# Emitting the next token group's load and normalization in pieces between the pieces of the current group's projections

## The chip, the cores and the metric

One Trainium2 chip, all 8 of its cores, one launch. Each core runs the same program on its own share and never waits for another. The metric is device time in microseconds (us) of the slowest core. The engines are TensorE (PE), VectorE (DVE), ScalarE (ACT), GpSimd (POOL) and SyncE (SP, which only issues DMAs here); each takes its instructions in order.

## The reference

One transformer block on x of 4 x 4096 x 2048: latent attention, then a gated feed-forward with int8 weights.

```python
h = layernorm(x)
q = h @ Wq + bq
kv_latent = h @ Wdown            # 2048 -> 512
k = kv_latent @ Wk_up            # 512 -> 2048
v = kv_latent @ Wv_up
q, k = rope(q), rope(k)          # 16 heads of 128
attn = softmax(causal(q k^T / sqrt(128)))
x = x + layernorm((attn v) @ Wo + bo)
g = silu((layernorm(x) @ w_gate) * s_gate)
u = (layernorm(x) @ w_up) * s_up
x = x + layernorm(((g * u) @ w_down) * s_down)
```

## The kernel before

Two cores share a batch row: each computes k and v for all 4096 tokens of it, and q, attention and feed-forward for 2048 of them. The program runs through stages A (normalization, latent, k, v), B (q), C (attention), D (output projection) and E (feed-forward), with a barrier of all engines behind each. Only stage A is touched by the change.

The program is first written down as lists, one for each engine: every call of `st(engine, fn, waits, ...)` appends one operation to its engine's list with the semaphore values that it waits for, and the lists are replayed in that order. So the order in which the Python code calls `st` is the order of each engine's queue, DMAs of SyncE among them; there is no other scheduler. Slots carry the events of a tile's last producer and of its users. SyncE's DMAs use eight semaphores in turn, and each waits for the one eight before it.

Stage A goes over 8 token groups (NKG) of 512 tokens. For each group:

- front(kg): four token tiles of 128. For each: SyncE loads x (line 337, 1 MB); VectorE sums (348); ScalarE squares and accumulates (350); small operations on VectorE, POOL and ScalarE give mean, variance, root (362) and reciprocal (364); ScalarE writes the normalized tile in bf16 (368); SyncE sends a transposing DMA that puts it into the group's feature-major tile xnfm (378). At the end two stores of xnfm to xnf_scr, 1 MB each (393), which wait for all four transposes. x tiles, normalized tiles and xnfm are double-buffered; the statistics are not.
- back(kg): the down projection, 4 chunks of 16 matmuls (411), each cast on ScalarE (420); then k, 16 chunks of 4 matmuls (442), each with three VectorE operations for the rotation (468, 470, 477) and a POOL add into the staging tile kst (485), and two stores to k_scr by SyncE (502); then v, 16 chunks of 4 matmuls (442 as well), each copied by ScalarE into vst (455), and two stores to v_scr (502). The chunks use two PSUM banks in turn.

The loop is `for kg in range(NKG): front(kg); back(kg)`, at the end of stage A.

Of the kernel before, what the change touches and what calls it, by code (L numbers as in the profile page):

```python
# [24 lines left out]
NKG = 8  # L25
# [89 lines left out]
def prod_waits(*slots):  # L115
    ws = []
    for s in slots:
        ws.extend(s.users)
        ws.extend(s.ready)
    return ws  # L120


def cons_waits(*slots):
    ws = []
    for s in slots:
        ws.extend(s.ready)
    return ws


def build_program():  # L130
# [120 lines left out]
    if "A" in PHASES:  # L251
# [74 lines left out]
        def front(kg):  # L326
            kgp = kg % 2
            xnfm = xnfm2[kgp]
            s_xnfm = s_xnfm2[kgp]
            for tt4 in range(4):  # L330
                tpar = (kg * 4 + tt4) % 2
                xt, sxt = x_t[tpar], s_xt[tpar]
                xn, sxn = xn_tm[tpar], s_xntm[tpar]
                row0 = kg * 512 + tt4 * 128

                ev = st("Q", lambda q, xt=xt, row0=row0:
                        q.dma_start(xt, xin[row0:row0 + 128, :]),
                        waits=prod_waits(sxt), dma="dQ")
                sxt.produced(ev)

                ssum = st_s[:, 0:1]
                nmean = st_s[:, 1:2]
                ssq = st_s[:, 2:3]
                var = st_s[:, 3:4]
                sd = st_s[:, 4:5]
                rstd = st_s[:, 5:6]
                t1 = st_s[:, 6:7]
                ev1 = st("V", lambda v, xt=xt: v.reduce_sum(ssum, xt, axis=AX),
                         waits=cons_waits(sxt) + prod_waits(s_stats))
                ev2 = st("S", lambda s, xt=xt: s.activation(  # L350
                    sqs, xt, ACT.Square, accum_out=ssq),
                    waits=cons_waits(sxt) + [ev1])
                sxt.used(ev2)
                ev3 = st("V", lambda v: v.tensor_scalar(
                    nmean, ssum, -1.0 / DM, None, op0=ALU.mult), waits=[ev1])
                ev4 = st("V", lambda v: v.tensor_scalar(
                    var, ssq, 1.0 / DM, None, op0=ALU.mult), waits=[ev2])
                ev5 = st("G", lambda g: g.tensor_mul(
                    t1, nmean, nmean), waits=[ev3])
                ev6 = st("G", lambda g: g.tensor_sub(var, var, t1),  # L360
                         waits=[ev4, ev5])
                ev7 = st("S", lambda s: s.activation(
                    sd, var, ACT.Sqrt, bias=eps_s, scale=1.0), waits=[ev6])
                ev8 = st("V", lambda v: v.reciprocal(rstd, sd), waits=[ev7])
                nmr = st_s[:, 7:8]
                ev8b = st("G", lambda g: g.tensor_mul(nmr, nmean, rstd),
                          waits=[ev8])
                ev9 = st("S", lambda s, xt=xt, xn=xn: s.activation(
                    xn, xt, ACT.Identity, bias=nmr, scale=rstd),
                    waits=prod_waits(sxn) + [ev8b])  # L370
                sxt.used(ev9)
                sxn.produced(ev9)
                s_stats.produced(ev8)
                s_stats.used(ev9)

                if tt4 == 0:
                    xnfm_evs = []
                ev = st("Q", lambda q, xn=xn, tt4=tt4, xnfm=xnfm: q.dma_start(
                    xnfm[:, :, tt4 * 128:(tt4 + 1) * 128], xn, transpose=True),
                    waits=cons_waits(sxn) + (prod_waits(s_xnfm)  # L380
                                             if tt4 == 0 else []),
                    dma="dQ", xpose=True)
                sxn.used(ev)
                xnfm_evs.append(ev)
            s_xnfm.produced(xnfm_evs)
            ev_xnfm = xnfm_evs

            for half in range(2):
                def fn(q, half=half, kg=kg, xnfm=xnfm):
                    dap = bass.AP(xnf_scr.tensor,  # L390
                                  half * 8 * 128 * SEQ + kg * 512,
                                  [[SEQ, 128], [128 * SEQ, 8], [1, 512]])
                    return q.dma_start(dap, xnfm[:, half * 8:half * 8 + 8, :])
                ev = st("Q", fn, waits=list(ev_xnfm), dma="dQ")
                s_xnfm.used(ev)
                scr_slot["xnf"].produced(ev)

        def back(kg):
# [5 lines left out]
            for lc in range(4):  # L404
                bank = lc % 2
                pss, psa = ps_slot[bank], ps_ap[bank]

                def fn(t, lc=lc, psa=psa, xnfm=xnfm):
                    r = None
                    for fc in range(NH):  # L410
                        r = t.matmul(psa, wdn_s[:, fc, lc * 128:(lc + 1) * 128],  # L411
                                     xnfm[:, fc, :],
                                     start=(fc == 0), stop=(fc == NH - 1))
                    return r
                ev = st("T", fn, waits=prod_waits(pss) +
                        cons_waits(s_xnfm, s_wdn))
                pss.produced(ev)
                s_xnfm.used(ev)
                s_wdn.used(ev)
                evv = st("S", lambda s, lc=lc, psa=psa, kvl=kvl: s.copy(  # L420
                    kvl[:, lc, :], psa),
                    waits=cons_waits(pss) + (prod_waits(s_kvl)
                                             if lc == 0 else []))
                pss.used(evv)
                if lc == 3:
                    s_kvl.produced(evv)
                elif lc == 0:
                    s_kvl.users = []

            for which in ("k", "v"):  # L430
                wsl = s_wku if which == "k" else s_wvu
# [1 line left out]
                stg = kst if which == "k" else vst  # L433
                sstg = s_kst if which == "k" else s_vst
                for fc in range(NH):
                    bank = 2 + (fc % 2)
                    pss, psa = ps_slot[bank], ps_ap[bank]

# [58 lines left out]
                for half in range(2):  # L497
                    def fn(q, dst=dst, half=half, stg=stg, kg=kg):
                        dap = bass.AP(dst.tensor,
                                      half * 8 * 128 * SEQ + kg * 512,  # L500
                                      [[SEQ, 128], [128 * SEQ, 8], [1, 512]])
                        return q.dma_start(dap, stg[:, half * 8:half * 8 + 8, :])
                    ev = st("Q", fn, waits=cons_waits(sstg), dma="dQ")
                    sstg.used(ev)
                    scr_slot[sname].produced(ev)

        for kg in range(NKG):
            front(kg)
            back(kg)

        plan.barrier()

# [771 lines left out]
```

How the kernel before makes its waits and increments, by code:

```python
    def replay(self, eng_handle, eng_name, sems):  # L85
        cur = {}
        for ws, fn, sem, inc in self.ops[eng_name]:
            for s, v in ws:
                if cur.get(s, 0) < v:
                    eng_handle.wait_ge(sems[s], v)
                    cur[s] = v
            if fn is None:
                continue
            inst = fn(eng_handle)
            if inc:
                inst.then_inc(sems[sem], inc)
```

## Time and profile before

| | us |
|---|---|
| median of 3 runs | 6654.31 |
| lowest run | 6634.15 |
| profiled execution, device time | 6641.46 |
| its span on the slowest core (core 2) | 6639.9 |
| spans of all cores | 6587.8 to 6639.9 |
| granted TensorE clock, all cores | 0.836 to 0.840 |

| stage | from, to (us of the span) |
|---|---|
| tables and weight preparation | 0 to 160 |
| stage A, first x load to last v store | 160 to 1315 |
| stage B | 1315 to 1600 |
| the rest | 1600 to 6640 |

PE is busy for 66% of the span, DVE 24%, ACT 20%, POOL 12%. A busy share is an average over stages with different limits, and stage A is where the page's slices show PE at 3 to 5 tenths. Durations of matmuls in the page overlap each other; their start-to-start distance is what they cost.

### The profile page before, as it was taken

To read this page: it belongs to the slowest core of one execution; us is meant where nothing else is said; L and a number is where in the kernel's file an instruction comes from. 1 tells how busy PE (TensorE), PEld (TensorE's weight loads), DVE (VectorE), ACT (ScalarE), POOL (GpSimd) and SP (SyncE) were. 2 spreads that over 40 slices of the span, in tenths; PEclk is the share of its full clock that TensorE was granted. 3 is DMA by queue.
4 is the path that set the end of the run, shared out by engine and by line. 5 is a ranking of instruction groups with operands and counts; after the bars stand their busy time and mean duration, and the time that the engine had idled before them with its cause. 6 is when DMAs were issued, how large, how long until landed. Compare 5 with 4: busy or idle time off the path is not lost.

```text
span 6639.9 us, 67786 instructions; the slowest of 8 cores (6587.8 to 6639.9 us)
## 1 busy us (share of the span) xinstructions
PE 4399.2 (66%) x21376; PEld 2013.5 (30%) x21376; DVE 1584.7 (24%) x2965; ACT 1349.2 (20%) x3067; POOL 818.8 (12%) x924
## 2 busy tenths in 40 slices
PE   0333434358566666663332999879986999869986
PEld 0111111123233333331111444334432444324432
DVE  0222333235233333323332111021102111021101
ACT  0222112111565666631111000011100100010000
POOL 0111111124000000000000111111111111111111
PEclk9866767679677666776776999989998999989998
DMA  9333323351777777774436997499956997489944
GB/s 187 94 86 91 86 76 89 105 111 39 164 151 149 154 153 149 149 160 127 139 114 129 153 153 142 127 165 152 146 140 153 154 153 133 128 162 152 153 122 131
DMA packets 1566328, 883.21 MB, mean 133 GB/s; under 512 B 777122, under 2 KB 1541026, under 8 KB 1550242
## 3 DMA queue, kind: packets, MB, share of 16 engines
q0 software_dynamic: 679296, 434.14, 38.2%
q1 hardware_dynamic: 839842, 327.28, 22.1%
q10 hardware_dynamic: 46848, 117.45, 5.3%
q8 instruction: 187, 3.06, 0.2%
q14 instruction: 155, 1.27, 0.1%
HBM read 398.53 MB, written 109.05 MB: 76 GB/s over the span
## 4 chain that ended last, share of the span: by engine, by line
PE 45%; DMA 19%; DVE 11%; ACT 11%; issue 8%; POOL 3%; SPq 2%; another core or an unknown queue 1%; ACTq 0%; DVEq 0%; POOLq 0%
PE ps L1029 13%; PE ps L1043 13%; PE ps L1096 8%; DMA arena<-wd 7%; ACT arena L764 7%; DMA ctxr<-xin 3%; PE ps L862 3%; PE ps L411 2%; PE ps L442 2%; PE ps L736 2%; DVE smalls L758 2%; POOL arena L619 2%; DMA arena<-arena 2%; DVE arena L477 1%; PE ps L697 1%
## 5 line engine op out<-in xcount | busy, mean ns | idle before, releaser
L1029 PE MATMUL ps<-arena 128*128 128x512 bf16 x4096 | 933.1, 381 | 265.4 <-DMA arena<-wg 142.5
L1096 PE MATMUL ps<-arena 128*128 128x512 bf16 x4096 | 916.5, 380 | 141.1 <-DMA arena<-wd 140.0
L1043 PE MATMUL ps<-arena 128*128 128x512 bf16 x4096 | 925.8, 379 | 0.0
L764 ACT ACTIVATE arena<-ps,smalls 128x512 bf16<-128x512 f32 (+1 forms) x1152 | 747.7, 666 | 461.6 <-DVE smalls L758 331.1
L736 PE MATMUL ps<-arena 128*128 128x512 bf16 (+1 forms) x1152 | 486.5, 485 | 418.6 <-ACT arena L764 337.7
L411 PE MATMUL ps<-arena 128*128 128x512 bf16 x512 | 128.8, 419 | 762.8 <-DMA arena<-ctxr 762.8
L1029 PEld LDWEIGHTS ps<-arena 128*128 128x128 bf16 x4096 | 402.1, 98 | 755.3 <-issue 277.1
L1096 PEld LDWEIGHTS ps<-arena 128*128 128x128 bf16 x4096 | 387.1, 98 | 669.9 <-issue 239.5
L1059 DVE TENSOR_SCALAR ctxr<-ps,smalls 128x512 bf16<-128x512 f32 x256 | 192.2, 751 | 1499.2 <-PE ps L1043 1499.2
L1043 PEld LDWEIGHTS ps<-arena 128*128 128x128 bf16 x4096 | 400.8, 98 | 483.2
L1054 ACT ACTIVATE ctxr<-ps,smalls 128x512 bf16<-128x512 f32 x256 | 175.9, 687 | 1562.6 <-PE ps L1029 1562.5
L862 PE MATMUL ps<-arena 128*128 128x512 bf16 x1024 | 227.7, 386 | 335.2 <-DMA arena<-wo_scr 306.7
L697 PE MATMUL ps<-arena 128*128 128x128 bf16 x4352 | 402.9, 267 | 30.2 <-DMA arena<-arena 22.6
L697 PEld LDWEIGHTS ps<-arena 128*128 128x128 bf16 x4352 | 364.6, 123 | 74.4 <-issue 63.3
L442 PE MATMUL ps<-arena 128*128 128x512 bf16 x1024 | 288.3, 419 | 126.5 <-DVE arena L477 116.1
L736 PEld LDWEIGHTS ps<-arena 128*128 128x128 bf16 x1152 | 117.4, 109 | 728.7 <-issue 721.9
L411 PEld LDWEIGHTS ps<-arena 128*128 128x128 bf16 x512 | 53.5, 106 | 837.6 <-issue 789.0
L585 PE MATMUL ps<-arena,ctxr 128*128 128x512 bf16 x1024 | 230.8, 390 | 113.6 <-DMA arena<-xnf_scr 85.2
L1085 POOL DMA_DIRECT2D arena<-wd x256 | 189.7, 741 | 943.6 <-PE ps L1096 932.0
L1019 POOL DMA_DIRECT2D arena<-wg x128 | 146.3, 1143 | 1165.2 <-PE ps L1029 1158.6
L1116 DVE TENSOR_TENSOR ctxr<-ps,ctxr 128x512 f32<-128x512 f32 x64 | 43.9, 691 | 1010.5 <-PE ps L1096 1010.3
L1148 ACT ACTIVATE sqs<-ctxr 128x2048 bf16<-128x2048 f32 x16 | 30.5, 1909 | 1166.8 <-DVE smalls L1145 1166.8
(74 smaller groups left out, 2781.5 us busy)
## 6 DMA issues: line engine op xcount, KB each, us to landing
arena<-wg POOLq DMA_DIRECT2D x128, 1024.0 KB, 6.8
arena<-wu POOLq DMA_DIRECT2D x128, 1024.0 KB, 7.1
arena<-wd POOLq DMA_DIRECT2D x256, 512.0 KB, 3.8
ctxr<-xin SPq DMA_DIRECT2D x32, 1024.0 KB, 5.9
arena<-wo_scr ACTq DMA_DIRECT2D x16, 2048.0 KB, 10.4
xnf_scr<-arena SPq DMA_DIRECT2D x16, 1024.0 KB, 7.1
k_scr<-ctxr SPq DMA_DIRECT2D x16, 1024.0 KB, 7.1
v_scr<-ctxr SPq DMA_DIRECT2D x16, 1024.0 KB, 7.5
```

Of the source, the lines that this page charges most:

```text
L411: r = t.matmul(psa, wdn_s[:, fc, lc * 128:(lc + 1) * 128], xnfm[:, fc, :], start=(fc == 0), stop=(fc == NH - 1))
L442: r = t.matmul(psa, wts[:, lc, fc * 128:(fc + 1) * 128], kvl[:, lc, :], start=(lc == 0), stop=(lc == 3))
L585: rr = t.matmul(psa, wq_s[:, fc, oc * 128:(oc + 1) * 128], xnfmB[:, fc, :], start=(fc == 0), stop=(fc == NH - 1))
L697: r = t.matmul(cpa[:, 0:128], PT_b[par][:, kc, :], v_t[hp][:, kc, :], start=(kc == 0), stop=(kc == W // 128 - 1))
L736: t.matmul(psa[:, 0:N], q_s[hp][:, tt * 128:(tt + 1) * 128], k_s[hp][:, n0:n0 + N], start=True, stop=True),
L764: s.activation(P_b[par][:, n0:n0 + N], psa[:, 0:N], ACT.Exp, bias=negc[:, par:par + 1], scale=1.0, accum_out=lacc[:, par * 8 + ci: par * 8 ...
L862: r = t.matmul(psa, ctxfm[tp][:, fc, j * 128:(j + 1) * 128], wo_s[wop][:, fc, :], start=(fc == 0), stop=(fc == NH - 1))
L1029: rr = t.matmul(ga, wg_s[slp][:, fc, icw * 128:(icw + 1) * 128], x1nfm[:, fc, :], start=(fc == 0), stop=(fc == NH - 1))
L1043: rr = t.matmul(ua, wu_s[slp][:, fc, icw * 128:(icw + 1) * 128], x1nfm[:, fc, :], start=(fc == 0), stop=(fc == NH - 1))
L1059: ev2 = st("V", lambda v, ic=ic, ua=ua: v.tensor_scalar(u_sb, ua, su_s[:, ic:ic + 1], None, op0=ALU.mult), waits=cons_waits(ub) + prod_wai ...
L1085: return g.dma_start(wd_s[qp], sap)
L1096: rr = t.matmul(psa, f_b[:, quar * 4 + ic, j * 128:(j + 1) * 128], wd_s[qp][:, ic, :], start=(quar == 0 and ic == 0), stop=(quar == 15 and ...
```

## The change

front and back become generators. front yields behind each token tile, and its two xnf stores come after the fourth yield. back yields behind the down projection, in the middle of k, behind the k stores, in the middle of v and behind the v stores. The driver runs front(0) by itself, and then for each group takes a piece of back(kg) and a piece of front(kg + 1) in turn. No operation, tile, wait rule or size differs; only the order in which the operations are put into the engines' lists.

```diff
@@ front(kg)
                 sxn.used(ev)
                 xnfm_evs.append(ev)
+                yield
             s_xnfm.produced(xnfm_evs)
             ev_xnfm = xnfm_evs
@@ back(kg)
                 elif lc == 0:
                     s_kvl.users = []
+            yield
 
             for which in ("k", "v"):
...
                 for fc in range(NH):
+                    if fc == 8:
+                        yield
                     bank = 2 + (fc % 2)
...
                     sstg.used(ev)
                     scr_slot[sname].produced(ev)
-
+                yield
+
+        def run_all(g):
+            for _ in g:
+                pass
+
+        fr = front(0)
+        run_all(fr)
+        fr = front(1) if NKG > 1 else iter(())
         for kg in range(NKG):
-            front(kg)
-            back(kg)
+            bk = back(kg)
+            while True:
+                try:
+                    next(bk)
+                except StopIteration:
+                    break
+                try:
+                    next(fr)
+                except StopIteration:
+                    pass
+            run_all(fr)
+            fr = front(kg + 2) if kg + 2 < NKG else iter(())
```

## Rows read from the trace of the kernel before

**Rows 1.** The page, costliest groups: busy, mean ns, idle before and its releaser.

```profile
L411 PE MATMUL ps<-arena 128*128 128x512 bf16 x512 | 128.8, 419 | 762.8 <-DMA arena<-ctxr 762.8
L442 PE MATMUL ps<-arena 128*128 128x512 bf16 x1024 | 288.3, 419 | 126.5 <-DVE arena L477 116.1
```

**Rows 2.** Table of stages: front(1), then down, k, v of back(1).

```profile
core 2: us, PE busy (x) PEld busy (x) DVE busy (x) ACT busy (x) POOL busy (x), PEclk, DMA share, GB/s
304.00:378.00 74.00, 0.31 (x1) 0.14 (x2) 11.03 (x16) 17.56 (x16) 2.30 (x12) 0.52 0.42 114
...
382.00:394.00 12.00, 11.87 (x55) 5.15 (x53) 0.00 (x0) 1.79 (x4) 0.00 (x0) 0.99 0.23 78
394.00:430.00 36.00, 21.23 (x68) 6.18 (x68) 32.57 (x48) 0.55 (x1) 19.03 (x15) 0.86 0.00 0
430.00:446.00 16.00, 14.50 (x62) 4.91 (x60) 0.53 (x1) 9.19 (x16) 1.27 (x1) 1.00 0.40 131
```

**Rows 3.** Timeline of PE: start, duration, what; first down matmuls of groups 1, 7.

```profile
377.69 16.18 PE L411 MATMUL ps<-arena 128*128 128x512 bf16 x64 [74.72 <-DMA arena<-ctxr]
...
1238.56 15.83 PE L411 MATMUL ps<-arena 128*128 128x512 bf16 x64 [75.65 <-DMA arena<-ctxr]
```

**Rows 4.** Timeline of SyncE's queue, from group 1's down projection to front(2).

```profile
377.63 1.03 SPq L393 DMA_DIRECT2D xnf_scr<-arena  x2
432.02 0.99 SPq L502 DMA_DIRECT2D k_scr<-ctxr  x2
446.29 1.00 SPq L502 DMA_DIRECT2D v_scr<-ctxr  x2
447.40 1.36 SPq L337 DMA_DIRECT2D ctxr<-xin  x1
465.96 1.48 SPq L378 DMA_TRANSPOSE arena<-ctxr  x1
```

**Rows 5.** Timeline of all engines, one token tile of front(0).

```profile
189.61 2.29 DVE L348 TENSOR_REDUCE smalls<-ctxr 128x1 f32<-128x2048 f32 x1 [10.88 <-DMA ctxr<-xin]
...
195.13 0.16 DVE L364 RECIPROCAL smalls<-smalls 128x1 f32<-128x1 f32 x1 [0.89 <-ACT smalls L362]
...
195.73 2.09 ACT L368 ACTIVATE ctxr<-ctxr,smalls 128x2048 bf16<-128x2048 f32 x1 [0.69 <-POOL smalls L366]
```

**Rows 6.** Timeline of PE's weight loads at the start of group 2's down projection.

```profile
520.17 0.15 PEld L411 LDWEIGHTS ps<-arena 128*128 128x128 bf16 x1 [0.28 <-issue]
520.60 0.15 PEld L411 LDWEIGHTS ps<-arena 128*128 128x128 bf16 x1 [0.27 <-issue]
...
525.64 4.42 PEld L411 LDWEIGHTS ps<-arena 128*128 128x128 bf16 x21 [0.20 <-issue]
```

**Rows 7.** Timeline of ACT in back(1): last down cast, first and last v copy.

```profile
393.96 0.58 ACT L420 CAST arena<-ps 128x512 bf16<-128x512 f32 x1 [2.87 <-PE ps L411]
430.42 0.58 ACT L455 CAST ctxr<-ps 128x512 bf16<-128x512 f32 x1 [35.87 <-PE ps L442]
...
445.59 0.58 ACT L455 CAST ctxr<-ps 128x512 bf16<-128x512 f32 x1 [0.50 <-PE ps L442]
```

**Rows 8.** Chain of waits, in order of time: front(2)'s first load.

```profile
447.40 9.91 DMA ctxr<-xin
```

**Rows 9.** Table of 2 us stretches (columns as in rows 2), behind the v stores.

```profile
450.00:452.00 2.00, 0.00 (x0) 0.00 (x0) 0.00 (x0) 0.00 (x0) 0.00 (x0) 0.61 1.07 343
```

**Rows 10.** Timeline of all engines in group 0's k: two chunks' first rotation, one add.

```profile
252.94 0.69 DVE L468 TENSOR_TENSOR arena<-ps,arena 64x512 f32<-64x512 f32 x1 [25.03 <-PE ps L442]
...
255.08 0.69 DVE L468 TENSOR_TENSOR arena<-ps,arena 64x512 f32<-64x512 f32 x1
255.20 1.27 POOL L485 TENSOR_TENSOR ctxr<-arena 128x512 bf16<-128x512 f32 x1 [26.96 <-DVE arena L477]
```

**Rows 11.** Time to landing: the 32 transposes (line 378), then the 32 x loads (line 337).

```profile
DMA to landing us min/median/max: 4.2/4.3/4.8
...
DMA to landing us min/median/max: 5.5/5.9/11.7
```

## The prediction, made before the changed kernel ran

> **What bounds the kernel now.** The page comes first, for the costly groups with idle time in front of them. The down projection (line 411) is busy for 128.8 us but has 762.8 us of idle time before it, nearly all of it ended by the transposing DMA that front() sends last; the up projection (line 442) has 126.5 us [rows 1]. The table of stages then shows one token group of stage A: 74 us in which TensorE does next to nothing (0.31 us busy), while VectorE and ScalarE are busy 11 and 17.6 us; then 12 and some us of down projection, 36 us of k with VectorE busy 32.6 of them, and 16 us of v with TensorE busy 14.5 [rows 2]. So a group is a front of about 74 us and a back of about 69 us, in turn. The first down matmul of groups 1 and 7 starts at 377.69 and 1238.56 us, a period of (1238.56 - 377.69) / 6 = 143.5 us [rows 3].
>
> Why they take turns is seen in SyncE's queue: the k stores and v stores wait for the staging tiles, and the next group's first x load stands right behind them, at 447.40; each later load stands behind a transpose that waits for its normalized tile (465.96) [rows 4]. The other engines are in order as well. One token tile of front is a chain over four engines: the sum starts at 189.61, the reciprocal ends at 195.29 (5.7 us, all of which VectorE's queue spends inside it), the normalized tile is ready at 197.82 (8.2 us after the sum's start; ScalarE is in it from 2.4 to 8.2) [rows 5]. Neither of the two halves saturates an engine over the whole period. The stages behind A are not touched, and start after a barrier.
>
> **The change, part by part.** No instruction is added or removed; five pieces of back(kg) alternate with five pieces of front(kg+1). I call them B1 (down), F0, B2 (k 0 to 7), F1, B3 (k 8 to 15, k stores), F2, B4 (v 0 to 7), F3, B5 (v 8 to 15, v stores), F4 (xnf stores). Every engine gets its share of them in this order, SyncE too. I lay out one steady period, t = 0 at the first down matmul.
>
> B1. TensorE comes from B5 at full clock. The spacing of weight loads is 0.43 us at the start of a down projection and 4.42 / 21 = 0.21 us later [rows 6], so 64 matmuls end at 13.8; the last of the four casts (0.58 us, on ScalarE, just behind the last matmul) ends at about 14.5 [rows 7]. v_scr stores are issued at 0.8, the xnf stores (F4) behind them, then the load of F0 at 2.9.
>
> F0. Today that load lands 11.0 us after the first v store's issue: 446.29 to 447.40 + 9.91 [rows 4, 8]. Now the xnf stores, 2.10 MB, are between them; at the 343 GB/s of a stretch with stores in flight [rows 9] they take 6.1 us. Landing: 0.8 + 11.0 + 6.1 = 17.9. The sum starts at 18.1, VectorE is through at 23.8, the tile is ready at 26.3. By the Trainium skill (DMA: Bandwidth & Descriptors, Where 436 GB/s comes from) HBM gives a core about 358 GB/s; 5.2 MB by that are 14.6 us, which would put the landing near 17 and the sum 1 us lower. The trace's 343 GB/s agrees.
>
> B2. VectorE spends 2.14 us on one k chunk (252.94 to 255.08), POOL's add 1.27 behind it [rows 10]. Eight chunks: 23.9 to 41.1. F1's load is issued at 28.3, behind the transpose, and lands 5.9 us later, at about 34.5 [rows 11]: hidden. F1: VectorE 41.1 to 46.8, tile ready at 49.3. B3: 46.9 to 64.1; last add done at 65.5.
>
> F2. k stores are issued at 65.6, F2's load right behind. The same pair as v stores and load today: 11.0 us, so 76.7. Sum at 76.8, tile ready at 85.0. This is the largest stall: VectorE idles 12.6 us. TensorE has v chunks 0 and 1 in its two banks and waits, because B4's copies are behind F2's work in ScalarE's queue.
>
> B4. Copies from 85.1. Today sixteen copies go from 430.42 to 446.17, 1.0 us each, TensorE at 1.00 clock [rows 2, 7]. After a pause of 20 us it will be at half clock: in the trace it is down to 0.61 granted between 450 and 452, some 5 us after its last matmul [rows 9]; there a chunk costs 4 x 0.43 = 1.7 us. Three of the six remaining chunks at 1.7 and three at 0.98: 8.1 us, TensorE through at 93.8, copies at 94.5. F3's load: issued at 87.2, lands at 93.1: hidden but for F3 itself. The Trainium skill (TensorE: Matmul & The Clock Gate, HAM oscillation — how this bites in real kernels) says that a loop which idles TensorE for a transfer in each pass starts each pass cold; by that all twelve chunks after the two pauses cost 1.7 and the period is 4.4 us longer.
>
> F3, B5. Sum at 93.2, tile ready at 101.4. The transpose lands 4.3 us after issue [rows 11], by 106, before B5 is through. Copies from 101.5, six chunks again at mixed clock: TensorE through at 110.2. Then B1 of the next group with no pause.
>
> Period 110.2 against 143.5: 33.3 us less, in seven periods 233. The first is some 4 us shorter (no v stores ahead of its load); the last back starts its down projection warm, some 2 us. Sum 239. The profiled execution took 6641.5 us (span 6639.9), 13 below the median and 7 above the lowest run: 6641.5 - 239 = 6402. I say 6405.
>
> **Costs that the trace does not show,** bounded from both sides. The F0 load behind 4.2 MB of stores: if the xnf stores cost nothing extra it lands at 11.8, but ScalarE is only free of B1's casts at 14.5, so VectorE would be through at 18.0, 5.8 us earlier; if they cost twice what I take, 6 us later. The value in the middle is the bandwidth of the nearest row. The F2 load: the slowest landing today is 11.7 us instead of 9.9 [rows 11], so up to 2 us later each, and 4 if the next front's transfers meet it; none earlier, the same pair is in the trace. Clock of the twelve chunks: all warm -4.5, all cold +4.4. SyncE's issue time is in the trace (0.5 us a store) and counted. Adding up, the period is 100 to 125: gains of 310 to 135, times of 6332 to 6507. These ends need all terms at once to go one way.
>
> **The rivals.**
> (a) Forecast: two short fronts hidden in the k half, the other two partly exposed; 6405. For it: SyncE's and the engines' orders are fixed by the code, all durations but one are rows.
> (b) Loads late. If the burst of stores holds up both loads that follow stores (F0, F2) by 7 us each, the period is 124 and the time 6641 - 7 x 19.5 - 6 = 6499. For it: behind two stores a landing takes 9.9 us and up to 11.7, against a median of 5.9 [rows 8, 11], and now four stores stand ahead of F0's load. Against it: 7 us more is over twice the bandwidth cost of what is added.
> (c) Full head-of-line blocking, no gain: each front's chain sits inside all four in-order queues, so that nothing runs beside it. Period: four tiles of 5.9 landing, 8.2 chain and some 2 us of issue (64), 69 of back, 9 for twelve cold v chunks: 142, so 6640. Against it: load times (5.9 of each 16) and the 1.8 us transpose issues don't occupy VectorE or ScalarE, and during B1 TensorE needs only ScalarE's four casts.
> (d) Slower. Transposes or loads get slow beside stores and compute. From 110 it takes 33 us per group to be at par, 52 to be 2% slower; three loads (F0, F2, F3) have no slack and F1 has 6.6 us, so par is at 11 us more for each of the three, and 2% slower at (52 + 6.6) / 4 = 15 us more for all four: landings of some 20 us where today's median is 5.9. Against it: transposes land in 4.2 to 4.8 us today although an x load is always issued right behind them [rows 4, 11].
> (e) Everything at its good end, clock up and store bursts hidden: 6345.
>
> **How the numbers follow.** (a) 0.70, (b) 0.13, (c) 0.04, (d) 0.03, (e) 0.10. The forecast is that of (a). The range takes in (a) with its own spread (6365 to 6450) and most of (e) and half of (b): 6350 to 6480. 2% is 133 us, about what a measurement of this kernel tells from no change for sure: 19 us per group. (a) and (e) are beyond it, (b), at 142 us gained, is close to the line: two thirds of it count as faster. Faster 0.90, same 0.07, slower 0.03.
>
> **What would show it.** Starts of the first down matmul 107 to 114 us apart; idle time before line 411 near zero but for the first group; new idle time before line 442's matmuls, some 20 us and 6 us per group, ended by ScalarE's copies; VectorE's wait for the load of F2 near 12 us, of F0 a few us, of F1 none; granted clock at 1.00 from the first down matmul of a group on, where it now starts at half. A load after v stores landing past t = 24, or copies of v that run at 1.7 us throughout, would make it wrong upward; down matmuls that don't directly follow the v matmuls would show that the last transposes are late, which I take not to happen.

## The result and the profile after

| | before | after |
|---|---|---|
| profiled execution, device time, us | 6641.46 | 6410.41 |
| span of its slowest core, us | 6639.9 | 6408.8 |
| first down matmul to first down matmul, mean of the seven periods, us | 143.3 | 109.8 |
| ratio of times, 95% interval | | 0.9623 (0.9565 to 0.9681) |

The changed kernel is faster by 3.8%. In some executions of either kernel the cores of one die, or of both, run at a lower granted clock, which puts the plain medians of ten runs at 6618.06 after and 6844.54 before, the first of them outside the range that was given; the ratio and the comparisons below are of executions without that (five of after: 6399.11 to 6417.14 us), or of cores of the other die.

The page of the changed kernel, costliest groups, and then the groups by line of stage A alone. Line 412 is the down projection (411 before), 446 the k and v chunks (442 before).

```profile
L412 PE MATMUL ps<-arena 128*128 128x512 bf16 x512 | 113.6, 383 | 234.6 <-DMA arena<-ctxr 234.6
```

```profile
L446 PE MATMUL ps<-arena 128*128 128x512 bf16 x1024 | 337.3, 477 | 385.3 <-DVE arena L481 189.6 <-ACT ctxr L459 186.9 <-ACT arena L421 6.7
```

Against [rows 1], the idle time before the down projection fell from 762.8 to 234.6 us, and those 234.6 are one wait, the way to the very first matmul. The idle time before k and v rose from 126.5 to 385.3. So 528 us went at one place and 259 came back at another. Of the second number 186.9 us is TensorE waiting for v's copies on ScalarE (line 459), where before it was 0.4 us; VectorE's part rose from 116.1 to 189.6. The difference of the two numbers is 269 us; the matmuls of both lines together were busy for 451 us instead of 417 [rows 1], 34 us more, as k and v now run at half clock more often. That leaves some 235 us, which is what stage A became shorter by.

The timeline of PE over one steady group shows where the idle time is:

```profile
340.73 13.98 PE L412 MATMUL ps<-arena 128*128 128x512 bf16 x64
355.53 1.89 PE L446 MATMUL ps<-arena 128*128 128x512 bf16 x8 [0.82 <-ACT arena L421]
367.52 1.87 PE L446 MATMUL ps<-arena 128*128 128x512 bf16 x4 [10.11 <-DVE arena L481]
...
390.65 1.87 PE L446 MATMUL ps<-arena 128*128 128x512 bf16 x4 [6.72 <-DVE arena L481]
...
427.30 10.29 PE L446 MATMUL ps<-arena 128*128 128x512 bf16 x32 [19.40 <-ACT ctxr L459]
443.59 7.26 PE L446 MATMUL ps<-arena 128*128 128x512 bf16 x24 [6.00 <-ACT ctxr L459]
450.69 4.48 PE L412 MATMUL ps<-arena 128*128 128x512 bf16 x20
```

Four pauses, one for each token tile: 10.1 and 6.7 us in k, 19.4 and 6.0 in v. The down projection of the next group starts right behind v, at 450.69. VectorE's sums (line 348) of the four tiles, on its timeline:

```profile
359.43 2.29 DVE L348 TENSOR_REDUCE smalls<-ctxr 128x1 f32<-128x2048 f32 x1 [29.32 <-DMA ctxr<-xin]
...
382.57 2.28 DVE L348 TENSOR_REDUCE smalls<-ctxr 128x1 f32<-128x2048 f32 x1
...
418.37 2.29 DVE L348 TENSOR_REDUCE smalls<-ctxr 128x1 f32<-128x2048 f32 x1 [12.58 <-DMA ctxr<-xin]
...
434.65 2.29 DVE L348 TENSOR_REDUCE smalls<-ctxr 128x1 f32<-128x2048 f32 x1 [10.60 <-DMA ctxr<-xin]
```

Only the second has no wait for its load. SyncE's queue over the same group:

```profile
341.65 1.03 SPq L506 DMA_DIRECT2D v_scr<-ctxr  x2
342.88 4.43 SPq L394 DMA_DIRECT2D xnf_scr<-arena  x2
347.40 3.75 SPq L337 DMA_DIRECT2D ctxr<-xin  x1
...
407.33 1.01 SPq L506 DMA_DIRECT2D k_scr<-ctxr  x2
408.49 1.26 SPq L337 DMA_DIRECT2D ctxr<-xin  x1
```

The load of tile 2 stands at 408.49, behind the k stores; that of tile 0 behind four stores. The table of stages for the down projection and the k and v parts (columns as in [rows 2]):

```profile
341.00:355.00 14.00, 13.71 (x64) 6.02 (x62) 0.00 (x0) 2.53 (x5) 0.00 (x0) 1.00 0.94 293
...
407.00:427.00 20.00, 0.90 (x3) 0.00 (x0) 2.75 (x4) 4.82 (x6) 0.77 (x4) 0.50 0.47 157
427.00:443.00 16.00, 10.16 (x32) 3.46 (x32) 2.76 (x4) 8.57 (x13) 0.57 (x3) 0.71 0.37 99
```

### The profile page after: what moved, and what is told of

Same layout as the page of the kernel before. It is cut to its first block, busy times and chain, and to the rows that moved or that the text cites. A ratio compares the mean times of both kernels' runs of the same rounds, so it can differ in the third digit from the quotient of the medians.

```text
span 6408.8 us, 67760 instructions; the slowest of 8 cores (6363.4 to 6408.8 us)
## 1 busy us (share of the span) xinstructions
PE 4460.7 (70%) x21376; PEld 2028.1 (32%) x21376; DVE 1583.6 (25%) x2965; ACT 1347.1 (21%) x3067; POOL 818.8 (13%) x924
## 4 chain that ended last, share of the span: by engine, by line
PE 44%; DMA 19%; DVE 11%; ACT 10%; issue 9%; POOL 3%; SPq 2%; another core or an unknown queue 1%; ACTq 1%; DVEq 0%; POOLq 0%
PE ps L1051 14%; PE ps L1065 14%; PE ps L1118 8%; DMA arena<-wd 8%; ACT arena L786 7%; PE ps L884 4%; DMA ctxr<-xin 3%; PE ps L758 2%; DMA arena<-arena 2%; POOL arena L641 2%; PE ps L719 2%; DVE smalls L780 2%; DVE arena L481 1%; DMA arena<-wo 1%
## 5 line engine op out<-in xcount | busy, mean ns | idle before, releaser
L1051 PE MATMUL ps<-arena 128*128 128x512 bf16 x4096 | 935.0, 382 | 260.1 <-DMA arena<-wg 136.7
L1118 PE MATMUL ps<-arena 128*128 128x512 bf16 x4096 | 926.7, 381 | 148.3 <-DMA arena<-wd 146.3
L1065 PE MATMUL ps<-arena 128*128 128x512 bf16 x4096 | 925.8, 379 | 0.0
L1051 PEld LDWEIGHTS ps<-arena 128*128 128x128 bf16 x4096 | 402.7, 98 | 751.2 <-issue 274.2
L446 PE MATMUL ps<-arena 128*128 128x512 bf16 x1024 | 337.3, 477 | 385.3 <-DVE arena L481 189.6
L1118 PEld LDWEIGHTS ps<-arena 128*128 128x128 bf16 x4096 | 387.3, 98 | 687.0 <-issue 261.8
L1065 PEld LDWEIGHTS ps<-arena 128*128 128x128 bf16 x4096 | 400.8, 98 | 483.3
L884 PE MATMUL ps<-arena 128*128 128x512 bf16 x1024 | 232.0, 391 | 321.9 <-DMA arena<-wo_scr 296.7
L719 PEld LDWEIGHTS ps<-arena 128*128 128x128 bf16 x4352 | 368.1, 123 | 78.2 <-issue 66.5
L758 PEld LDWEIGHTS ps<-arena 128*128 128x128 bf16 x1152 | 118.1, 109 | 725.4 <-issue 720.7
L607 PE MATMUL ps<-arena,ctxr 128*128 128x512 bf16 x1024 | 230.8, 390 | 110.5 <-DMA arena<-xnf_scr 83.7
L446 PEld LDWEIGHTS ps<-arena 128*128 128x128 bf16 x1024 | 100.4, 112 | 622.2 <-issue 584.9
L412 PE MATMUL ps<-arena 128*128 128x512 bf16 x512 | 113.6, 383 | 234.6 <-DMA arena<-ctxr 234.6
```

Source lines behind the costliest of these rows:

```text
L446: r = t.matmul(psa, wts[:, lc, fc * 128:(fc + 1) * 128], kvl[:, lc, :], start=(lc == 0), stop=(lc == 3))
L607: rr = t.matmul(psa, wq_s[:, fc, oc * 128:(oc + 1) * 128], xnfmB[:, fc, :], start=(fc == 0), stop=(fc == NH - 1))
L719: r = t.matmul(cpa[:, 0:128], PT_b[par][:, kc, :], v_t[hp][:, kc, :], start=(kc == 0), stop=(kc == W // 128 - 1))
L758: t.matmul(psa[:, 0:N], q_s[hp][:, tt * 128:(tt + 1) * 128], k_s[hp][:, n0:n0 + N], start=True, stop=True),
L884: r = t.matmul(psa, ctxfm[tp][:, fc, j * 128:(j + 1) * 128], wo_s[wop][:, fc, :], start=(fc == 0), stop=(fc == NH - 1))
L1051: rr = t.matmul(ga, wg_s[slp][:, fc, icw * 128:(icw + 1) * 128], x1nfm[:, fc, :], start=(fc == 0), stop=(fc == NH - 1))
```

## The experiments

Two theories stood against each other. Mine: the gain has two parts, front's chain running beside the projections and loads whose transfer time is now covered by other work; what is left is three late loads plus a ScalarE chain ahead of v's copies. The rivals: only one of the two parts counts; or the stalls that are left belong to the in-order queues and not to the loads. Seven kernels tell them apart. Only the order of operations changes in them, and in the last the PSUM banks of v as well. Periods are the mean of seven, unless one period is named. They are read from a kernel's line on its down projection, where the last start is the 64th matmul of group 7, 13.8 us (15.8 where that group starts at half clock) behind its first: (last start - first start - 13.8) / 7, good to 0.1 us.

**Early loads in the kernel before.** No interleaving; each load is issued one tile earlier:

```diff
+        def xload(i):
+            if i >= NKG * 4:
+                return
+            xt, sxt = x_t[i % 2], s_xt[i % 2]
+            ev = st("Q", lambda q: q.dma_start(xt, xin[i * 128:i * 128 + 128, :]),
+                waits=prod_waits(sxt), dma="dQ")
+            sxt.produced(ev)
+        xload(0)
...
-                ev = st("Q", lambda q, xt=xt, row0=row0: ...)
-                sxt.produced(ev)
+                xload(kg * 4 + tt4 + 1)
```

> The kernel before with one edit and no interleaving: each x load is issued one tile earlier, ahead of the transpose of the tile before it, so the first load of a group stands ahead of the k and v stores. Theory (the changed kernel gains by running front's chain beside the projections as well as by hiding loads): here only the landing times go, 5.9 us of tiles 1 to 3 with some 2 us of issue, and 11 us of tile 0, partly given back as load 1 now stands behind the v stores; with VectorE's first sum done beside v, the period falls from 143.5 to about 111 us, so the kernel is near 6415, about as fast as the changed kernel, and the two gains must be largely different ones, to be added in the next run. Rival (the gain comes from engines working beside each other, loads matter little): period above 130, time above 6550.

The line on its down projection, and the timeline of PE:

```profile
L417 PE MATMUL ps<-arena x512: 379/379/634, 210.4 to 1005.3; 128*128 128x512 bf16 x171
...
322.48 15.47 PE L417 MATMUL ps<-arena 128*128 128x512 bf16 x64 [42.95 <-DMA arena<-ctxr]
```

Period 111.3 us; 6388.85 us in the profiled execution, a single one without a ratio, beside 6630.25 to 6642.74 of before. TensorE's wait for the front fell from 74.7 us [rows 3] to 43.0. The rival is out: moving loads by one tile in SyncE's queue is worth as much as the whole change. The time is 26 us below what I wrote, because front(0) got shorter too: the first down matmul starts at 210.4 instead of 235. I had counted periods only.

**Early loads in the changed kernel.** The same diff on top of the change.

> The changed kernel with the same early loads. Theory: the stall before the sum of tile 2 (12.6 us of VectorE, behind the k stores) and that of tile 0 (behind v and xnf stores) go, and the period falls from 110.5 to about 90: sum of tile 0 before B1, VectorE through with it at 18.0 (ScalarE's casts bind), tile 2 ready at 66.4, v chunks 8 to 15 from 82. Time about 6265. Rival (the stalls are the in-order queues', not the loads'): the sums start earlier but TensorE's pauses of 19.4 and 6.0 us before v chunks stay as they are, period 105 or more, time above 6370.

The timeline of PE over one period:

```profile
302.87 13.98 PE L418 MATMUL ps<-arena 128*128 128x512 bf16 x64
...
369.86 10.27 PE L452 MATMUL ps<-arena 128*128 128x512 bf16 x32 [7.56 <-ACT ctxr L465]
385.32 7.47 PE L452 MATMUL ps<-arena 128*128 128x512 bf16 x24 [5.18 <-ACT ctxr L465]
392.62 13.98 PE L418 MATMUL ps<-arena 128*128 128x512 bf16 x64
```

Period 89.9, ratio to before 0.9406 (0.9383 to 0.9428), 6224.26 us in the profiled execution. TensorE's pause ahead of v chunk 2 fell from 19.4 to 7.6 us: the 11.8 us that went were the wait for the load. What stays, 7.6 and 5.2, is ScalarE's chain in front of v's copies. The time is 41 us below what I wrote; some 25 of them are again the shorter front(0), which I had not counted. The four periods make a table:

| | loads where they were | loads one tile early |
|---|---|---|
| front, then back | 143.3 | 111.3 |
| pieces alternating | 109.8 | 89.9 |

Either edit alone is worth 32 to 33.5 us a group, both 53.4: some 12 us are hidden by either of them.

**All four tiles in the k half.**

```diff
-                    if fc == 8:
+                    if which == "k" and fc in (4, 8, 12):
                         yield
...
-                yield
+                if which == "k":
+                    yield
```

> The changed kernel with other places for the pieces: k is cut behind chunks 4, 8, 12 and 16 and v is not cut, so all four token tiles lie in the k half, the xnf stores behind the k stores. Theory: ScalarE's chain no longer stands ahead of v's copies, and no load stands behind four stores; TensorE's pauses inside v (19.4 and 6.0 us) vanish, in their place VectorE pauses for loads 1 to 3 by 2 us each; v runs in 15 to 17 us. Period about 91, time about 6275. Rival (VectorE is the limit and the two halves are balanced as they are): four tiles of 5.7 us more in the k half cost what v gains, period 105 to 115, time 6370 to 6440.

The line on its down projection (core 2), and the timeline of PE around v:

```profile
L412 PE MATMUL ps<-arena x512: 379/379/634, 244.8 to 906.7; 128*128 128x512 bf16 x171
...
414.30 14.71 PE L446 MATMUL ps<-arena 128*128 128x512 bf16 x60 [1.12 <-DVE arena L481]
428.85 11.39 PE L412 MATMUL ps<-arena 128*128 128x512 bf16 x52
```

v runs through in 14.7 us, without the 19.4 and 6.0. Period 92.6, 6287.5 us in the profiled execution (no ratio), against 91 and 6275. But the edit moves two things at once. No tile stands ahead of v's copies any more; and no x load stands behind the k stores or the xnf stores. The next two kernels do the second alone, one load each, for 11.6 and 3.7 of the 17.2 us. So most of this gain can be had from the loads, and the place of the tiles is priced only by khalf_ahead against inter_ahead, below.

**k stores behind tile 2's load.** Only this moves:

```diff
+                    def issue(fn=fn, sstg=sstg, sname=sname):
+                        ev = st("Q", fn, waits=cons_waits(sstg), dma="dQ")
+                        sstg.used(ev)
+                        scr_slot[sname].produced(ev)
+                    if which == "k" and kg < NKG - 1:
+                        pend.append(issue)
+                    else:
+                        issue()
...
                 sxt.produced(ev)
+                while tt4 == 2 and pend:
+                    pend.pop(0)()
```

> The changed kernel with one thing moved: the two k stores stand behind the x load of tile 2 in SyncE's queue instead of ahead of it. Nothing else is earlier. Theory (the largest stall that is left is that load's wait for the k stores: issued after kst is full and landing behind 2.1 MB): the load is issued right behind tile 1's transpose, at about 52 us of the period, and lands at 58, so tile 2's sum starts when VectorE is through with k, at 64 instead of 77.6, and all that follows is 12 to 13 us earlier: period 97 to 98.5 against 110.2, TensorE's pause before v chunk 2 falls from 19.4 to 6 or 7 us, time about 6322. Rival (ScalarE's chain ahead of v's copies is the stall, the load only fills it): pause of 15 us or more, period above 105.

The timelines of PE and of DVE's sum of tile 2:

```profile
329.04 13.98 PE L416 MATMUL ps<-arena 128*128 128x512 bf16 x64
...
403.18 9.84 PE L450 MATMUL ps<-arena 128*128 128x512 bf16 x32 [6.72 <-ACT ctxr L463]
...
427.60 13.98 PE L416 MATMUL ps<-arena 128*128 128x512 bf16 x64
...
394.26 2.28 DVE L352 TENSOR_REDUCE smalls<-ctxr 128x1 f32<-128x2048 f32 x1
```

Tile 2's sum starts 394.26 - 329.04 = 65.2 us into the group, without a wait, instead of 77.6. The pause is 6.7 instead of 19.4, the steady period 98.6 (98.2 over all seven), the time 6311.37 in the profiled execution and 6314.86 in another. The ratio is 0.9588, but its interval, 0.9295 to 0.9881, is too wide to call it a gain of 2% or more, so this too rests on the period. 12 us a group of the changed kernel's period was this one place in SyncE's queue.

**xnf stores behind the next group's first load.** The two stores of front(kg) are kept back and issued behind the x load of tile 0 of front(kg + 1):

```diff
+            def xnf_stores(s_xnfm=s_xnfm, ev_xnfm=ev_xnfm, xnfm=xnfm):
...
+            pend.append(xnf_stores)
...
                 sxt.produced(ev)
+                if tt4 == 0 and pend:
+                    pend.pop(0)()
```

> The changed kernel with the two xnf stores of a group moved behind the x load that follows them (the next group's first). Theory (that load is late by the bandwidth of 2.1 MB ahead of it): sum of tile 0 at 12 instead of 18.7 after the first down matmul, bound by ScalarE's casts after that, VectorE through 5.5 us earlier, period 104 to 105, time about 6375. Rival (the burst as a whole is slow, or later loads pay for it): period within 1.5 us of 110.5 with the loads of tiles 0 or 1 landing late all the same.

The sum of tile 0 in the group whose first down matmul is at 342.69, and the down projection's line (core 3):

```profile
356.10 2.29 DVE L352 TENSOR_REDUCE smalls<-ctxr 128x1 f32<-128x2048 f32 x1 [24.49 <-DMA ctxr<-xin]
...
L420 PE MATMUL ps<-arena x512: 379/379/634, 234.9 to 991.3; 128*128 128x512 bf16 x171
```

The sum starts at 13.4 instead of 18.7, where 12 was expected; period 106.1, 3.7 less than the change's (4.8 to 5.8 were expected), ratio to before 0.9605 (0.9581 to 0.9628), times 6370.49 and 6377.00. The interval of the ratio overlaps the change's own, so it is the period that shows the gain. That 2.1 MB ahead of a load cost it 5.3 us bears out the size that the prediction took from a bandwidth row (6.1).

**Both edits that worked.** Early loads and four tiles in the k half.

> The two edits that each worked, together: x loads one tile early, and all four token tiles in the k half. Theory (with loads hidden and v left alone, VectorE is the limit between B1 and v): VectorE through with tile 0 at 18, then four times 8.6 us of chunks and three times 5.7 us of tiles: 69.5, then v in 15: period 84.5 to 86, against 89.9 and 92.4 for either edit alone; time about 6190. Rival (the two edits hide the same time): period 89 or more, time above 6215.

The timeline of PE, two down projections in turn (core 4):

```profile
300.84 13.98 PE L418 MATMUL ps<-arena 128*128 128x512 bf16 x62
386.16 13.98 PE L418 MATMUL ps<-arena 128*128 128x512 bf16 x63
```

These two are 85.3 apart; the mean of the seven is 85.7, ratio 0.9360 (0.9340 to 0.9380), 6211.32 us in the profiled execution. The period is as expected; the time was expected at 6190, and the 21 us between were not traced. Over inter_ahead's 89.9 the gain is 4.2 us: that is what the place of the tiles is worth by itself, once the loads are early in both. A tile in the middle of v puts ScalarE's chain ahead of the copies, but with early loads the pauses are 7.6 and 5.2 us only.

**k and v chunks side by side.** ScalarE has little to do in k and VectorE little in v. So chunk fc of k (banks 2 and 3) is followed by chunk fc of v (banks 4 and 5); loads are early, tiles behind the down projection and chunks 4, 8, 12:

```diff
-            for which in ("k", "v"):
+            for fc in range(NH):
+                if fc in (4, 8, 12):
+                    yield
+                for which in ("k", "v"):
...
-                    bank = 2 + (fc % 2)
+                    bank = (2 if which == "k" else 4) + (fc % 2)
```

> x loads one tile early, and k and v chunks side by side: chunk fc of k (banks 2, 3), then chunk fc of v (banks 4, 5), with the front tiles behind the down projection and behind chunks 4, 8 and 12; all four stores at the end. Theory (what remains after hiding loads is that VectorE idles in v and ScalarE in k): v's 15 us go beside k, period 18 + 4 x 8.6 + 3 x 5.7 = 69.5 plus up to 5 for v chunks whose copies wait behind ScalarE's chain and for matmuls at half clock after VectorE's 5.7 us pauses: 70 to 75, time about 6110. Rival (TensorE, in order and often at half clock, becomes the limit: 8 matmuls of 0.43 us a chunk pair are 3.4 us against VectorE's 2.14): period 88 or more, no gain over 6220.

The timeline of PE over one period (core 3):

```profile
280.32 16.98 PE L418 MATMUL ps<-arena 128*128 128x512 bf16 x64
298.12 4.36 PE L452 MATMUL ps<-arena 128*128 128x512 bf16 x16 [0.82 <-ACT arena L427]
...
317.76 9.66 PE L452 MATMUL ps<-arena 128*128 128x512 bf16 x32 [5.48 <-DVE arena L487]
332.52 10.54 PE L452 MATMUL ps<-arena 128*128 128x512 bf16 x32 [5.11 <-DVE arena L487]
348.16 5.58 PE L452 MATMUL ps<-arena 128*128 128x512 bf16 x16 [5.10 <-DVE arena L487]
353.57 6.74 PE L418 MATMUL ps<-arena 128*128 128x512 bf16 x25
```

This one period is 73.3, the mean of the seven on this core 74.2; ratio to before 0.9200 (0.9180 to 0.9220), times 6110.69 and 6111.95 us. This is the fastest version: a further 4.4% off the changed kernel's ratio of 0.9623 (0.920 / 0.9623 = 0.956). TensorE pauses for 5.1 to 5.5 us at each of three tiles, while VectorE is inside front's chain, and hardly elsewhere. The rival (TensorE at half clock is the limit, 88 or more) is out, but TensorE's clock does show: this down projection takes 17.0 us where the others took 14.0. The table of stages for core 3:

```profile
260.00:335.00 75.00, 57.38 (x196) 21.70 (x195) 44.80 (x66) 28.38 (x36) 23.01 (x29) 0.74 0.64 171
```

The granted clock is 0.74 over these 75 us, and 0.81 in the down projection itself (280.3 to 297.3). On core 0 of the same execution it is 0.87 from 210 to 720 us, the down projection that starts at 281.14 takes 13.98, and the mean period is 72.0. So the lower clock goes with some 2 us a group here.

## Why the prediction was right and where it failed, point by point

**The step that failed** is the one from the period to the time: "The profiled execution took 6641.5 us (span 6639.9), 13 below the median and 7 above the lowest run: 6641.5 - 239 = 6402." It takes one profile for the kernel's time, and puts at nothing what the cores lose when they are granted a lower clock. The three runs behind that median were 6634.15, 6654.31 and 7103.41 us, so even they spread by 469 us. Over ten runs the median stands 203 us above the profiled execution before (6844.54 and 6641.46) and 208 us after (6618.06 and 6410.41), and 6618.06 is 138 us above the upper end of the range. In an execution of the changed kernel that took 6853.61 us, cores 0 and 1 were granted 0.777 and 0.775 and had spans of 6852.0 and 6848.7; cores 4 to 7 of the same launch were granted 0.848 to 0.852 and had 6380.7 to 6397.8. Neither the range nor any rival has a term for that. Why a die is granted less in one execution and not in the next, no run here shows. The difference between the kernels is hardly touched by it: 231 us between the profiled executions and 226 between the medians of ten, where the sum had 239.

The mechanism was the one forecast, and 6405 us stands beside 6410.41 of the profiled execution. The ledger of one period, in us from its first down matmul, read off the rows above (group at 340.73):

| step | predicted | measured |
|---|---|---|
| down projection at full clock | 13.8 | 13.98 |
| sum of tile 0 | 18.1 | 359.43 - 340.73 = 18.7 |
| sum of tile 1, no wait for its load | 41.1 | 382.57 - 340.73 = 41.8 |
| sum of tile 2 | 76.8 | 418.37 - 340.73 = 77.6 |
| sum of tile 3 | 93.2 | 434.65 - 340.73 = 93.9 |
| next down projection | 110.2 | 450.69 - 340.73 = 110.0 |

The events run late by 0.6 to 0.8 us from the first sum on, and the last one is right because v chunks 8 to 15 took that back: only two of them ran at half clock, not three. That end is in part luck.

**The load behind four stores** was the one term with a bandwidth in place of a duration: landing 17.1 us after the first v store's issue. It landed at 347.40 + 11.80 = 359.20, 17.6 us after 341.65. The chain of waits has that load, and then that of tile 2:

```profile
347.40 11.80 DMA ctxr<-xin
...
408.49 9.72 DMA ctxr<-xin
```

Its issue was not where the ledger had it: 6.7 us into the period (347.40 - 340.73) instead of 2.9, since SyncE took 4.43 us over the two xnf stores, where the prediction had counted 0.5 us a store. The landing moved by 0.6 us at most (18.5 against 17.9).

The Trainium skill (DMA: Bandwidth & Descriptors, Where 436 GB/s comes from) puts HBM at some 358 GB/s a core. An estimate from that figure, 14.6 us for all 5.24 MB from the first store's issue at 0.8, is 15.4 us of the period, and not the "near 17" of the prediction, which its numbers don't give. The landing was at 18.5, which is 299 GB/s over those 5.24 MB. What came out right was to take a landing that the trace has and to add only the 2.10 MB that are new; for these alone 358 or 343 GB/s makes a difference of 0.3 us, which decides nothing.

**The clock in v.** Three of six chunks at half clock were taken after each pause. ScalarE's copies on its timeline:

```profile
429.25 0.59 ACT L459 CAST ctxr<-ps 128x512 bf16<-128x512 f32 x1 [1.72 <-PE ps L446]
430.96 0.59 ACT L459 CAST ctxr<-ps 128x512 bf16<-128x512 f32 x1 [1.12 <-PE ps L446]
432.67 0.59 ACT L459 CAST ctxr<-ps 128x512 bf16<-128x512 f32 x1 [1.12 <-PE ps L446]
433.78 0.59 ACT L459 CAST ctxr<-ps 128x512 bf16<-128x512 f32 x1 [0.53 <-PE ps L446]
```

1.71 us apart for the first three, then 1.1 and less: three after the long pause, two after the short one (445.55 to 447.04 is 1.5, then 0.9). The Trainium skill (TensorE: Matmul & The Clock Gate, HAM oscillation — how this bites in real kernels) says that a loop which idles TensorE for a transfer starts each pass cold. The trace agrees for the start; that a piece stays cold to its end, which would have cost 4.4 us, it does not show.

**First and last periods.** The first was to be some 4 us shorter: 340.73 - 234.65 = 106.1, against 110.5 for the mean of the other six. Stage A's last v stores are issued at 1070.54 on core 1 of after and at 1307.25 on core 2 of before:

```profile
1307.25 1.00 SPq L502 DMA_DIRECT2D v_scr<-ctxr  x2
```

236.7 us earlier, where the sum had 239. The span of the slowest core fell by 231.1; the other 5.6 us lie behind stage A, in stages that are the same and on another core. The cores differ by more than that: on core 1 of both kernels the stores are 235.1 us earlier (1305.63 before) and the span is 223.3 shorter, while the medians of the two dies fell by 247.2 and 235.1.

**The signs.** The starts are 106.1 to 111.7 apart on core 1, the idle time before line 412 is that of the first group alone, the pauses in v are 19.4 and 6.0, and the granted clock is 1.00 in the down projection. One sign was misnamed. VectorE's wait for the load of F0 was to be "a few us" and is 29.3; the ledger itself gives 110.2 + 18.1 - 98.9 = 29.4, as VectorE has nothing to do between the chain of F3 and that sum. What is a few us is how far the load holds back the chain beyond ScalarE's casts.

**The rivals.** (c), no overlap, and (d), slower, are out: the period is 33.5 us shorter. (d) needed landings of some 20 us for four x loads of a group; they land in 5.5 to 13.1 us, median 6.1, and the transposes in 4.3 to 5.9. (b), loads late by 7 us, is out: counted from the first store's issue, the load of F0 landed 0.5 us late and that of F2 0.1 us early (408.49 + 9.72 - 407.33 = 10.9, where the ledger had 11.0). Of (e), nothing showed: the clock did fall and the store burst wasn't hidden. What the ledger did not see is that the same gain was to be had without any interleaving, by moving the loads alone.

## What to carry to other kernels

When stages of a software pipeline are emitted in pieces into in-order queues, write down one period engine by engine, DMA issue queue included, with the durations of the old trace; here that gave each of six events within 0.8 us. Look first at what stands ahead of each load in the issuing queue: a load that has its buffer free but stands behind a store that waits for a result cost 12 us a group at one place here. Moving loads in the queue gave as much as the interleaving, and is the smaller edit. Then put the pieces where the engine that the inserted chain occupies is the bound anyway, not where it stands ahead of another engine's evictions; that was worth another 4.2 us a group. And a period that is right does not make the time right: the base has to come from the spread of the kernel's runs, which here was 469 us in three, and not from one profile.

## What the runs showed of the hardware that was not expected

SyncE's own issue time is not constant. Before, the two xnf stores were issued in 1.03 us and an x load in 1.36 [rows 4]; behind the v stores the same two stores took 4.43 and the load 3.75. With early loads in the kernel before, a transpose that stands behind two stores and a load took 6.15 us to issue, against 1.6 to 2.0 for the next three; the timeline of SyncE's queue:

```profile
281.43 1.34 SPq L330 DMA_DIRECT2D ctxr<-xin  x1
286.01 6.15 SPq L384 DMA_TRANSPOSE arena<-ctxr  x1
```

These long issues all stand behind 2 to 4 MB that were issued a few us before, though a load right behind 2 MB took only 1.36 [rows 4]. One reading is that the issuing engine stands still until part of that is through, a limit on the outstanding work of the queue. That is argued from these durations and not shown: no run varied it by itself, and one transpose took 3.08 us (at 390.85 in the changed kernel) with no store issued near it. What the long issues cost was not measured by itself; the load of F0, issued 3.8 us later than forecast, landed 0.5 us late.
